# Second layer of eight experts as split products, with GpSimd making the low parts of the hidden activations

## The reference

```python
v = jnp.clip(x @ v_w + v_b, -V_MAX, V_MAX)
a = (-2.0 + v).astype(jnp.complex64) - 1j
G = bk_green_diag(a)                 # two scans over the 64 tokens of an image, d = a_i - 1/d
feats = jnp.stack([G.real, G.imag], axis=-1)
probs = jax.nn.softmax(x @ gate_w + gate_b, axis=-1)
topv, topi = jax.lax.top_k(probs, K) # K = 2, then normalised and spread to comb [.., 8]
h = jax.nn.gelu(jnp.einsum('bnd,edf->bnef', x, w1) + b1)
y = jnp.einsum('bnef,efd->bned', h, w2) + b2
ffn_out = jnp.einsum('bne,bned->bnd', comb, y)
return ffn_out + bk_scale * (feats_clipped @ out_w + out_b)
```

## Time and profile before

| | |
|---|---|
| median of 3 runs | 403.28 us (402.86 to 409.09) |
| the profiled execution | 402.34 us, span 400.6 us |
| PE busy | 381.1 us (95%) |
| DVE busy | 242.4 us (61%) |
| ACT busy | 174.0 us (43%) |
| POOL busy | 69.2 us (17%) |
| granted TensorE clock, mean | 0.991 of full speed |

### The profile page before, as it was taken

How to read it: one execution, slowest core, us unless ns; L and a number is a source line. 1 busy time by engine, 2 the same in 40 slices (tenths; PEclk the granted TensorE clock), 3 DMA queues, 4 the chain that set the end, 5 groups by cost and what they waited for, 6 DMA issues and landing times.

```text
span 400.6 us, 8785 instructions
## 1 busy us (share of the span) xinstructions
PE 381.1 (95%) x3602; PEld 312.7 (78%) x3602; DVE 242.4 (61%) x712; ACT 174.0 (43%) x304; POOL 69.2 (17%) x113
## 2 busy tenths in 40 slices
PE   8999999999899899979999899999999999999993
PEld 8988779779567566656557798899899898888783
DVE  1567756803499887896344568557558207676344
ACT  1256552561466666744435716225324310541420
POOL 7140010430023221331101400000000200304003
PEclk9999999999999999999999999999999999989997
DMA  8999800000259500000006984404401000000001
GB/s 205 263 202 218 176 15 2 1 2 0 53 171 269 136 2 2 2 4 2 2 0 176 269 227 139 130 11 137 139 7 53 2 0 2 2 2 2 0 2 39
DMA packets 28725, 30.69 MB, mean 77 GB/s; under 512 B 4867, under 2 KB 24137, under 8 KB 28686
## 3 DMA queue, kind: packets, MB, share of 16 engines
q1 hardware_dynamic: 28220, 29.96, 29.8%
q10 hardware_dynamic: 306, 0.17, 0.2%
q0 software_dynamic: 160, 0.01, 0.0%
HBM read 29.73 MB, written 0.39 MB: 75 GB/s over the span
## 4 chain that ended last, share of the span: by engine, by line
PE 77%; DVE 12%; ACT 4%; issue 4%; POOL 2%; DVEq 0%; POOLq 0%
PE ps L1529 68%; PE ps L1533 6%; PE ps L1541 4%; DVE front L1199 2%; DVE front L1189 2%; DVE front L1188 1%; DVE bn L1029 1%; POOL rstd L525 1%; DVE front L1177 1%; DVE wide L1394 0%; DVE xn L1044 0%; ACT front L687 0%; ACT front L805 0%; DVE front L1179 0%; DVE mv L1032 0%
## 5 line engine op out<-in xcount | busy, mean ns | idle before, releaser
L1529 PE MATMUL ps<-halves 128*128 128x512 f32 (+2 forms) x380 | 84.1, 376 | 1.3 <-ACT front L743 1.3
L1529 PEld LDWEIGHTS ps<-halves 128*128 128x128 f32 x380 | 66.6, 188 | 13.4 <-ACT front L743 1.7
L1529 PE MATMUL ps<-wide,front 128*128 128x192 f32 x432 | 72.0, 327 | 0.0
L1529 PEld LDWEIGHTS ps<-wide,front 128*128 128x128 f32 x432 | 70.3, 190 | 1.0 <-issue 0.5
L1529 PEld LDWEIGHTS ps<-front 64*32 64x32 f32 (+3 forms) x1488 | 51.4, 132 | 20.0 <-issue 11.6
L1529 PE MATMUL ps<-front 64*32 64x64 f32 (+3 forms) x1488 | 60.0, 241 | 5.8 <-issue 2.1
L743 ACT ACTIVATE front<-ps,colc 128x512 f32<-128x512 f32 x60 | 39.7, 688 | 53.8 <-PE ps L1529 53.7
L569 POOL TENSOR_TENSOR front<-front 128x768 f32<-128x768 f32 x16 | 23.6, 1472 | 75.8 <-DVE front L1200 75.8
L1332 DVE SCALAR_TENSOR_TENSOR xn<-ps,small,xn 128x192 f32<-128x192 f32 x28 | 9.8, 411 | 28.0 <-PE ps L1529 28.0
L1189 DVE TENSOR_TENSOR front<-front 128x768 f32<-128x768 f32 x16 | 23.9, 1493 | 0.5
L1529 PE MATMUL ps<-xT,turned 128*64 128x256 f32 (+1 forms) x96 | 22.6, 458 | 0.8 <-ACT front L781 0.8
(11 more groups left out here) (280 smaller groups left out, 553.3 us busy)
## 6 DMA issues: line engine op xcount, KB each, us to landing
wide<-in_w SPq DMA_DIRECT2D x8, 576.0 KB, 4.5
wide<-in_w SPq DMA_DIRECT2D x8, 384.0 KB, 5.7
wide<-in_w SPq DMA_DIRECT2D x16, 192.0 KB, 6.3
front<-in_a2w SPq DMA_DIRECT2D x5, 576.0 KB
front<-in_a1w SPq DMA_DIRECT2D x5, 384.0 KB
front<-in_x SPq DMA_DIRECT2D x3, 512.0 KB, 7.4
...
```

Source lines behind the costliest of these rows:

```text
L1529: return pe.matmul(o, l, r, start=start, stop=stop)
```

## The change

1. The second layer becomes a split product too. `hraw` holds the GELU's float32 result, ScalarE copies it to a high part (`hidden_high`), GpSimd subtracts to get the low part, one 128x512 tensor_tensor per tile, 48 in all. The weights get a high part from ScalarE (`w2_high`, 1152 columns) and a low part from VectorE (`w2_low`, 1152 columns), side by side in `w2x`. `down_split` multiplies the high hidden tile by high and low weights together (384 columns) and adds the low hidden tile by the first 256 of those columns: 48 fp32r matmuls per expert in place of 24 in float32.
2. A token tile's result now takes 384 columns of a bank, so one expert takes banks 4 to 7, and `weighted` runs eight times per expert, in two groups of four. down(d) waits for the sum of expert d-1.
3. `gates` makes the logits first; the exponential comes after the fourth GELU of expert 0. The turning of the gate weights and the extra products move into up(7), and wait there for the sum of expert 5.
4. In VectorE's iteration e the low weights `w1_low(e + 3)` and `w2_low(e + 2)` come behind the scan steps. The features come behind both.
5. The transfers of the scan move from GpSimd's queue to SyncE's. The class weights are loaded behind the stage: `a1w` once down(6) and the last low part are done, `a2w` after down(7), since the hidden buffers lie in their place.

```diff
--- before.py
+++ after.py
...
         a2w = take(5, NF, D)
+
+        halves_f = nc.alloc_sbuf_tensor_at("halves_f", [P, 22960], F32R, offset=front_at)
+        take = carve(halves_f)
+        hs = take(2, NF, 2, T)
+        raw_at = 2 * NF * 2 * T
+        take(3, T)
+        w2x = take(2, NF, 2 * D)
+        hraw = [turned[:, k * T:(k + 1) * T] for k in range(3)] + [
+            front[:, raw_at + k * T:raw_at + (k + 1) * T] for k in range(3)]
 
         take = carve(turned[:, xs_at + 4 * T:])
         km3 = take(2, B, 2, S)
...
+                if e == NSLOT:
+                    sp.wait_ge(s["chain_in"], 1)
+                    sp.dma_start(chA[0:8], vrow.rearrange("o (b n) -> o b n", n=S)).then_inc(s["rowmv_in"], 16)
+                    sp.dma_start(chA[8:16], vrev.rearrange("o (b n) -> o b n", n=S)).then_inc(s["rowmv_in"], 16)
...
-                    sp.wait_ge(s["y_mm"], e - NSLOT + 1)
+                    sp.wait_ge(s["w2_lo"], e - NSLOT + 1)
                 sp.dma_start(w2s[:, k], a["w2"][e].rearrange("(f p) n -> p f n", p=P)).then_inc(w2_in[k], 16)
...
+
+            sp.wait_ge(s["chain_in"], 2)
+            sp.dma_start(chE, chS[8:16]).then_inc(s["chE_in"], 16)
+            sp.wait_ge(s["feat_out"], 1)
+            for k in range(2):
+                sp.dma_start(frow[k:k + 1].rearrange("o (b n) -> o b n", n=S), chF[:, k, :]).then_inc(s["chF_in"], 16)
+            sp.wait_ge(s["y_mm"], EM - 1)
+            sp.wait_ge(s["h_lo"], NF * EM)
+            for x in range(5):
+                for c, (r0, n) in enumerate(CH):
+                    load(a1w[0:n, x, c], a["a1w"][x, r0:r0 + n], "a_in")
+            sp.wait_ge(s["y_half"], 2)
+            for x in range(5):
+                load(a2w[:, x], a["a2w"][x].rearrange("(f p) n -> p f n", p=P), "a_in")
+            sp.wait_ge(s["pad_made"], 6)
+            load(a1w[DB:DB + 1, :, 1, :], a["a1b"].rearrange("(o e) f -> o e f", o=1), "a_in")
...
+            tell(pool.memset(wg2[0:DB], 0.0), "pad_made")
+
+            for e in range(EM):
+                for f in range(NF):
+                    pool.wait_ge(s["h_hi"], NF * e + f + 1)
+                    h = hs[:, (e + 1) % 2, f]
+                    ins = pool.tensor_tensor(h[:, 1, :], hraw[f], h[:, 0, :].bitcast(F32), ALU.subtract)
+                    ins.then_inc(s["h_lo"], 1)
             pool.wait_ge(s["h_mm"], NF * (EM + 1))
             tell(pool.memset(g1T[0:DB], 0.0), "pad_made")
+            pool.wait_ge(s["h_lo"], NF * EM)
+            tell(pool.memset(vbd3, 0.0), "zeros_made")
+            pool.wait_ge(s["y_mm"], EM - 1)
+            tell(pool.memset(a1w[DB:P, :, 1, :], 0.0), "pad_made")
             norm()
...
-            for e in range(EM):
+
+            def w2_high(e):
+
+                act.wait_ge(w2_in[e % NSLOT], 16 * (e // NSLOT + 1))
                 if e >= 2:
                     act.wait_ge(s["y_mm"], e - 1)
-                hidden(hT[:, e % 2], R_MOE + NF * e, ACT.Gelu_apprx_tanh)
-                if e == 0:
-                    act.wait_ge(s["lg_sub"], 1)
-                    act.activation(lg, lg, ACT.Exp).then_inc(s["lg_exp"], 1)
+                act.activation(w2x[:, e % 2, :, 0:D], w2s[:, e % NSLOT], ACT.Copy).then_inc(s["w2_hi"], 1)
+
+            def expert_hidden(e, f):
+
+                bank = jobs[0] % 4
+                jobs[0] += 1
+                act.wait_ge(s["h_mm"], jobs[0])
+                if e >= 1:
+                    act.wait_ge(s["h_lo"], NF * (e - 1) + f + 1)
+                act.activation(hraw[f], ps[:, bank, :], ACT.Gelu_apprx_tanh,
+                               bias=col(R_MOE + NF * e + f)).then_inc(s["h_act"], 1)
+
+            def hidden_high(e, f):
+
+                act.wait_ge(s["h_act"], NF * (e + 1) + f + 1)
+                if e >= 2 and f == 0:
+                    act.wait_ge(s["y_mm"], e - 1)
+                act.activation(hs[:, (e + 1) % 2, f, 0, :], hraw[f], ACT.Copy).then_inc(s["h_hi"], 1)
+
+            w2_high(0)
+            for e in range(EM):
+                for f in range(NF):
+                    expert_hidden(e, f)
+                    if f >= 1:
+                        hidden_high(e, f - 1)
+                    if e == 0 and f == 3:
+                        act.wait_ge(s["lg_sub"], 1)
+                        act.activation(lg, lg, ACT.Exp).then_inc(s["lg_exp"], 1)
+                hidden_high(e, NF - 1)
                 if e + 2 < EM:
                     w1_high(e + 2)
+                if e + 1 < EM:
+                    w2_high(e + 1)
...
-                part_out(nth(5, j), j, xs, ((6, 5), (7, 2))[j], both_here=j == 0)
+                part_out(nth(5, j), j, xs, ((2, 5), (7, 2))[j], both_here=j == 0)
...
+
+            def w2_low(e):
+
+                dve.wait_ge(s["w2_hi"], e + 1)
+                w = w2x[:, e % 2]
+                dve.tensor_tensor(w[:, :, D:2 * D], w2s[:, e % NSLOT], w[:, :, 0:D].bitcast(F32),
+                                  ALU.subtract).then_inc(s["w2_lo"], 1)
+
+            w2_low(0)
...
+            def weighted(dst, src, e, i, part):
+                return dve.scalar_tensor_tensor(dst[:, i, :], ps[:, 4 + i, part * D:part * D + D], comb[:, i, e:e + 1],
+                                                src[:, i, :], ALU.mult, ALU.add)
+
+            w1_low(2)
+            w2_low(1)
+            for e in range(EM - 1):
                 dve.wait_ge(s["y_mm"], e + 1)
                 for i in range(NT):
-                    ins = weighted(xn, e, i)
+                    ins = weighted(xn, xn, e, i, 0)
+                link(ins)
+                for i in range(NT):
+                    ins = weighted(xn, xn, e, i, 1)
                 ins.then_inc(s["y_done"], 1)
                 dve.wait_ge(s["y_done"], e + 1)
-                if e == 0:
+                if e == EM - 3:
                     dve.wait_ge(s["combT_mm"], 1)
-                    dve.tensor_copy(combT[0:EM], ps[0:EM, 6, :]).then_inc(s["combT_done"], 1)
+                    dve.tensor_copy(combT[0:EM], ps[0:EM, 7, :]).then_inc(s["combT_done"], 1)
+                    dve.wait_ge(s["extra_mm"], 1)
+                    dve.tensor_tensor(xn2, xn2, two(4), ALU.add).then_inc(s["extra_done"], 1)
+                    dve.wait_ge(s["extra_done"], 1)
                 for n in range(FIRST + PER * e, min(S, FIRST + PER * (e + 1))):
                     chain_step(n)
+                if e + 3 < EM:
+                    w1_low(e + 3)
+                if e + 2 < EM:
+                    w2_low(e + 2)
                 if e == EM - 4:
                     chains_end()
-                    w1_low(EM - 1)
                     features()
...
-                weighted(tok, EM - 1, 2 * g)
-                link(weighted(tok, EM - 1, 2 * g + 1))
+                weighted(tok, xn, EM - 1, 2 * g, 0)
+                link(weighted(tok, xn, EM - 1, 2 * g + 1, 0))
+                weighted(tok, tok, EM - 1, 2 * g, 1)
+                link(weighted(tok, tok, EM - 1, 2 * g + 1, 1))
...
+            def down_split(e, tiles):
+
+                w, h = w2x[:, e % 2], hs[:, (e + 1) % 2]
+                for i in tiles:
+                    own = slice(i * P, (i + 1) * P)
+                    for f in range(NF):
+                        if i == 0:
+                            pe.wait_ge(s["h_lo"], NF * e + f + 1)
+                        mm(ps[:, 4 + i, 0:2 * D], h[:, f, 0, own], w[:, f, :], f == 0, False)
+                        ins = mm(ps[:, 4 + i, 0:256], h[:, f, 1, own], w[:, f, 0:256], False, f == NF - 1)
+                return ins
+
+            for e in range(EM):
+                pe.wait_ge(s["w1_lo"], e + 1)
...
+                    up(w1x[0], xs, range(4, NF))
+                elif e < EM - 1:
+                    up(w1x[e % 2], xs)
+                else:
+                    up(w1x[e % 2], xs, range(2))
+                    pe.wait_ge(s["y_done"], e - 1)
                     for i in range(NT):
...
+                        ins = tr(ps[0:EM, 7, i * P:(i + 1) * P], comb[:, i, :])
                     ins.then_inc(s["combT_mm"], 1)
...
+                    up(w1x[e % 2], xs, range(2, 4))
+                    pe.wait_ge(s["combT_done"], 1)
                     pe.wait_ge(s["chF_in"], 32)
...
+                        mm(two_t(4, i), combT[0:EM, i * P:(i + 1) * P], b2m[0:EM], True, False)
+                        ins = mm(two_t(4, i), frow[:, i * P:(i + 1) * P], ow3[0:3], False, True)
                     ins.then_inc(s["extra_mm"], 1)
+                    up(w1x[e % 2], xs, range(4, NF))
+                    pe.wait_ge(s["extra_done"], 1)
...
+                    pe.wait_ge(s["w2_lo"], e)
+                    if e == 1:
+                        pe.wait_ge(s["chain_in"], 1)
+                        pe.wait_ge(s["comb_done"], 1)
+                    if e >= 2:
+                        pe.wait_ge(s["y_done"], e - 1)
+                    down_split(e - 1, range(NT)).then_inc(s["y_mm"], 1)
+            pe.wait_ge(s["w2_lo"], EM)
+            pe.wait_ge(s["y_done"], EM - 1)
```

(3 more changed lines are left out.)

147 lines of the change are left out of this document (28 added, 119 removed).

## The result

The changed kernel takes **441.06 us** (median of 4 runs, 439.96 to 442.48) against 403.09 of the kernel before (4 runs): ratio 1.0943, 95% interval 1.0914 to 1.0971. One run of the kernel before, at 409.09, was in the slower state and is left out of the ratio. The prediction said 422, range 407 to 432. Its sign and its mechanism held, and its size did not: one term, the small operations of VectorE that wait for GpSimd (the scan steps above all), is 28 us and not 10. The profiled execution took 439.96.

What follows compares the result with a forecast made beforehand. The prediction took TensorE, executing or waiting without a break through the expert stage, as the bound. On 402.34 us it added 5.8 without contention, 10.0 held operations, 1.9 sum's wait and 2 clock, +19.7: 422 us, range 407 to 432.

Steps and rivals of the forecast that it cites:

- up(1)'s fifth tile starts later: Start of the expert stage: ScalarE's weight and hidden copies delay expert 1's first GELU, +1.9 us on TensorE.
- period of TensorE's own work: Expert loop: one expert's up and down on TensorE, without waits, takes 14.07 us instead of 14.63.
- up(7) late by held operations: Expert loop: scan operations on VectorE wait for GpSimd's subtractions, so up(7) starts 10.0 us late, worst 18.
- wait for expert 5's sum, with contention: In up(7): TensorE waits 6.8 us for VectorE's sum, instead of 4.9 without contention.
- down(6)'s end to the turn, at full clock: Tail: from down(6)'s end to the turn of the tokens takes 11.2 us, +2.9 over before.
- the clock: Behind the wait in up(7): matmuls start at half clock, 0 to 5 us, taken as +2.
- class weights: Loads moved behind down(6) and down(7): all there by 375, first use at 394, hidden with 19 us of cover.
- The forecast of 7.10 for a down: Second layer: 24 pairs of 384- and 256-column matmuls per expert take 7.10 us, 0.56 less than 7.66.
- the best case: VectorE's scan: one step passes per GpSimd operation, 5 of 10 steps delayed, 2.9 us lost per iteration.
- the case that the prediction called the worst: VectorE's scan: half a step passes per GpSimd operation, 7 steps delayed, 4.3 us lost per iteration.
- Rival 1: VectorE keeps up, the scan's tiny operations slipping past GpSimd: 408 us, 410 with the slow clock; chance 0.22.

Runs made afterwards that it cites:

- e1_tiny: Changed kernel with GpSimd's subtraction on 2 of 512 columns per tile, hidden-layer low parts left out: 411.99 us, ratio 1.0238.
- The three sizes: GpSimd's 512-column subtraction whole (changed kernel, 441.06 us), in two pieces of 256 columns (433.08 us) and in four of 128 (420.71 us).

## Why the prediction was right in kind and wrong in size

By its own terms, in us:

| step | predicted | measured |
|---|---|---|
| up(1)'s fifth tile starts later | +1.9 | +1.3 |
| period of TensorE's own work | 14.07 | 13.85, so 1.5 more gained |
| up(7) late by held operations | +10.0 (worst 18) | **+28.1** |
| wait for expert 5's sum, with contention | 6.8 | 6.9 |
| down(6)'s end to the turn, at full clock | 11.2 | 11.0 |
| the clock | +2 | +5.9 |
| class weights | hidden | hidden |

**Start.** The expected cause was there, ScalarE with its copies ahead of expert 1's GELUs, and a size was off. Against the last group of 256-column matmuls (212.73 in the timeline above), the fifth tile of up(1) starts after 15.76 us (228.49) and before after 14.51 (229.12, less 214.61). down(0) starts only 0.8 later (18.16 for 17.38), because the turns of the gate weights have left this place. Rows of the timeline of PE before:

```profile
214.61 2.64 PE L1529 MATMUL ps<-halves 128*128 128x256 f32 x20
...
231.99 7.97 PE L1529 MATMUL ps<-wide,front 128*128 128x192 f32 x48
```

This execution was lucky here. The wait ahead of the fifth tile is 2.57 us in every trace of the changed start; in eight of the eleven other traces the ten matmuls behind it ran slower (3.7 to 4.2 us for 2.57), and down(0) started after 19.2 to 19.8 us. As long as VectorE is late for up(2) this costs nothing.

**Down.** The experts of e1_tiny are 13.85 apart. The forecast of 7.10 for a down was good: 7.04 there (301.97 to 309.01). The split form does what it should.

**Held operations: the step that failed.** The mechanism was read rightly off L1189 and L525, and the two signs that the prediction asked for are there, operations far over 0.15 and 0.21 us, released at GpSimd's ends. Three inputs to its size were wrong. GpSimd's subtraction was taken as 1.03 us from an operation with a repeated operand; it is 1.27, so GpSimd runs 7.6 us with next to no gap. Second, the best case, "one step gets through per GpSimd operation", was taken as the likely one, on the idea that L1334 and the next L1331 fit one gap. They don't: the gap lets one through, and the other finds the next subtraction running (L1334 ends at 254.26 and L1331, from 254.30 on, waits until 255.53). The three sizes show half a step per instruction, the case that the prediction called the worst. Even that case was too low, at 4.3 us per iteration: with 1.27 in place of 1.03 it is 5.6. (The best case had a slip besides: five steps of 0.62 are 3.1 us, not 2.9.) VectorE's iteration is then 13.0 + 5.4 = 18.4, and the period 18.49.

Third, the start. With nothing held, up(2) could follow down(0) at 230.89 + 7.20 = 238.09, and up(7) five periods of 13.85 later, at 307.3. It starts at 335.45: 28.1 late, of which 4.9 fall ahead of up(2) and 4.6 on each of five periods. The prediction gave the start 1.4 on VectorE, for eight steps and the low weights, and nothing on TensorE. Against e1_tiny, and counted from the last group of 256-column matmuls, VectorE has the low weights for up(2) ready 9.6 us later: 3.7 of it in the eight steps, and 5.9 ahead of them, in operations that the prediction did not count at all. These are the gate chain (3.97 us for 0.63 in the row above), a two-input operation on the scan's input (L1326, 1.21 for 0.21) and copies of one input (L1300, 1.40 for 0.42; L1328, 1.09 for 0.16). VectorE had 4.7 us in hand there, so the eight steps alone would have cost TensorE nothing. The change itself put the gate chain there, ahead of the exponential's old place and beside the subtractions of expert 0.

e1_tiny confirms the sum. Counted in the same way its up(7) starts 26.7 us earlier; its own start was 1.3 us longer by the slow clock, which makes 28.

**The clock.** Predicted as a consequence of the wait, and it came: half clock until about 350. At 5.9 us it is beyond the 0 to 5 that was allowed: it is paid behind the wait in up(7), where it falls twice, and again in down(7), which takes 8.81 for 7.31.

**Sum's wait and tail.** The row of 344.64 shows 5.83 of idle time, because the ten matmuls ahead of it ran slower (3.36 us); from where they would have ended at full clock (335.45 + 2.33, the prediction's measure) it is 6.9. The wait and the tail both came out within 0.2 us, the wait partly by luck. From the end of `w1_low(7)` to the start of the sums it is 6.4 us for 6.3: the features took 3.1 and not 2.5, because one of them was held too (L1351, 0.85 for 0.21), and the transfer (1.84 of waiting) and `w2_low` took less than their terms.

**Class weights.** The loads start behind down(6), at 364.26, as predicted. They are through by 388, where the first use comes at 411.83, and nothing in the timeline of PE waits for them; from the turn to the end of the span it is 61.1 us (437.8 - 376.69) and was 61.7 (400.6 - 338.87). No kernel was run with this part alone, so this rests on the trace.

The errors add up: 18.1 for the held operations, 3.9 for the clock and 0.1 for the sum's wait, less 1.5 (period), 0.6 (start) and 0.2 (tail), is 19.8. Outside the stage this execution was 2.1 us shorter than the one before (1.9 of it ahead of the stage), which leaves 17.7. The profiled execution was at 439.96, 18.0 over the forecast.

Rival 1, that tiny operations slip past GpSimd, is refuted by every row of the scan that lies beside a subtraction. Its time, 408 to 410, is nearly that of the kernel with the two-column subtraction (412.0), as it should be.
